# Setup, attention's first batch and the second feed-forward's beginning placed anew: a macaron block (feed-forward, attention, feed-forward) on one core

## The reference

```
x = x + 0.5 * ffn(layernorm(x))        # router, 8 experts of at most 320 tokens, overflow goes to a dense MLP
x = x + attn(layernorm(x))             # 16 heads of 16 channels, 1024 x 1024 scores per head and batch
x = x + 0.5 * ffn(layernorm(x))        # the same ffn weights again
```

```
ffn:  eid = argmax(softmax(xf @ router_w + router_b));  rank = place among the tokens of the same expert
      rank < 320: relu(xf @ w1[eid] + b1[eid]) @ w2[eid] + b2[eid]
      else:       relu(xf @ ow1 + ob1) @ ow2 + ob2
attn: xd = x @ W_down; keys, queries, values = per-head 16x16 maps of xd
      softmax(queries keys^T * scale) values, then @ W_unify + b_unify
```

## Time and profile before

| | us |
|---|---|
| median of three runs | 2703.88 (2700.58 to 2704.08) |
| the profiled execution | 2695.95 |
| its span | 2694.2 |
| PE, DVE, ACT, POOL busy | 2582.5, 2052.0, 1761.2, 915.1 |
| granted TensorE clock, mean | 0.983 of full |

### The profile page before, as it was taken

How to read it: one execution, slowest core, us unless ns; L and a number is a source line. 1 busy time by engine, 2 the same in 40 slices (tenths; PEclk the granted TensorE clock), 3 DMA queues, 4 the chain that set the end, 5 groups by cost and what they waited for, 6 DMA issues and landing times. The chain is left out here.

```text
span 2694.2 us, 46722 instructions
## 1 busy us (share of the span) xinstructions
PE 2582.5 (96%) x17379; PEld 1624.1 (60%) x17379; DVE 2052.0 (76%) x3471; ACT 1761.2 (65%) x3620; POOL 915.1 (34%) x975
## 2 busy tenths in 40 slices
PE   6999999977999999999999999999999699999998
PEld 6888899952344344443443443444444488888998
DVE  5656557847898998998998989979997266655586
ACT  4444446743787887887877878878878444444576
POOL 2333324632332342333323323422212143332364
PEclk9999999986999999999999999999999799999999
DMA  4421214515244143242351341432421332221353
GB/s 121 97 71 56 64 53 126 160 56 97 49 78 104 48 94 78 62 100 57 78 103 52 72 103 49 81 74 66 81 60 43 112 87 74 61 71 40 86 156 96
DMA packets 191811, 216.86 MB, mean 80 GB/s; under 512 B 56364, under 2 KB 152804, under 8 KB 191584
## 3 DMA queue, kind: packets, MB, share of 16 engines
q1 hardware_dynamic: 156176, 169.03, 26.9%
q0 software_dynamic: 35408, 44.84, 6.0%
HBM read 114.54 MB, written 48.57 MB: 61 GB/s over the span
## 5 line engine op out<-in xcount | busy, mean ns | idle before, releaser
L1397 DVE TENSOR_REDUCE at_mxc<-at_pb 128x2 f32<-128x1024 f32 x1024 | 1210.7, 1219 | 137.6 <-PE at_pb L1227 134.4
L1337 ACT ACTIVATE at_ex<-at_pd 128x512 f32<-128x512 f32 (+1 forms) x2418 | 1105.8, 539 | 303.9 <-PE at_pd L1237 293.1
L1237 PE MATMUL at_pd<-at_qa,at_ka 50*128 50x512 f32 (+1 forms) x2418 | 641.1, 406 | 4.3 <-ACT at_ex L1337 4.3
L1237 PEld LDWEIGHTS at_pd<-at_qa,at_ka 50*128 50x128 f32 x2418 | 317.9, 185 | 493.1 <-issue 404.5
L1227 PE MATMUL at_pb<-at_ka,at_qa 48*128 48x512 f32 x2048 | 551.5, 467 | 33.5 <-DVE at_mxc L1397 17.7
L699 ACT ACTIVATE f_ml_h<-f_ml_pL,b1T 128x512 f32<-128x512 f32 (+1 forms) x384 | 243.6, 634 | 493.5 <-PE f_ml_pL L763 493.4
L614 DVE TENSOR_TENSOR f_ml_hl<-f_ml_h,f_ml_hh 128x512 fp32r<-128x512 f32 (+1 forms) x384 | 279.4, 728 | 364.5 <-ACT f_ml_hh L702 363.5
L1246 PE MATMUL at_po<-at_ex,at_va 128*32 128x512 f32 x4096 | 546.3, 605 | 0.0
L776 PE MATMUL f_ml_pA<-f_wh,f_ml_hh 128*128 128x256 f32 (+1 forms) x1408 | 411.5, 292 | 0.0
L778 PE MATMUL f_ml_pA<-f_wl,f_ml_hh 128*128 128x256 f32 (+1 forms) x1408 | 396.8, 282 | 0.0
L779 PE MATMUL f_ml_pA<-f_wh,f_ml_hl 128*128 128x256 f32 (+1 forms) x1408 | 396.8, 282 | 0.0
(11 more groups left out here) (123 smaller groups left out, 2645.7 us busy)
## 6 DMA issues: line engine op xcount, KB each, us to landing
f_wraw<-in_L_ffn_w SPq DMA_DIRECT2D x128, 256.0 KB, 3.2
at_qa<-at_parts SPq DMA_DIRECT2D x384, 64.0 KB, 2.5
at_ka<-at_parts SPq DMA_DIRECT2D x384, 64.0 KB, 2.6
at_oscr<-at_os POOLq DMA_DIRECT2D x63, 256.0 KB, 2.4
f_ml_xr<-in_L_attn_x SPq DMA_DIRECT2D x16, 512.0 KB, 6.7
f_ml_xs<-in_L_attn_x SPq DMA_DIRECT2D x16, 512.0 KB, 4.4
x<-f_ml_yo SPq DMA_DIRECT2D x16, 512.0 KB, 5.3
at_xr<-x SPq DMA_DIRECT2D x16, 512.0 KB, 4.8
```

What stands on the lines that cost most here:

```text
L1237: eng.matmul(pd[n.bank][:, part.at], ka[g][rows, p, kt * P:(kt + 1) * P], qa[g][rows, qh, p, part.at], start=True, stop=True).then_inc(s_f ...
L1337: eng.activation(ex[t % 2][:, part.j, part.at], pd[n.bank][:, part.at], ACT.Exp).then_inc(s_free[n.bank].sem, 1)
L1397: eng.tensor_reduce(mxc[:, t // NT, kh, t % NT::NT], pb[kh][:, :].rearrange("p (e k) -> p e k", e=2), AX.X, ALU.max, negate=True).then_inc ...
```

## The change

**Setup goes into the first feed-forward's block.** `setup` only notes its inputs. In `mlps` with `setup` given, SP issues the first rows, one piece of the weights and only then the biases; the router's and attention's weights come behind. POOL makes the constants at the start of the same block, PE turns the biases into a half of a tile of pA, DVE copies them out between its first statistics and its first weights. `turned(u, f)` sends the second turn of the first block to pR, so that it doesn't wait for pT.

**The second feed-forward's start goes into attention's last batch.** A `Shared` set of tiles (rows, raw weights, high and low weights) serves both. Attention's xr and xT lie in the raw weights' tile, its xn and xd in the rows' tile, its parts in the high and low weights' tiles. In batch 7 SP loads the dense weights and the first 512 rows at unit 1, step 0 (`load_next`); POOL splits the eight pieces at steps 2, 3, 10, 11 of units 1 and 2 (`next_split`); DVE and POOL do statistics, power and normalising of the first rows at steps 7, 8, 9 and 11 of unit 3. The second `mlps` (`early = 1`) leaves all of that out.

**Attention's first batch.** The list becomes `XT + XD[:2] + QK[:2] + XD[2:] + V + QK[2:]`. Its qk is split straight out of PSUM: ACT writes the high part, DVE the low (`queries_low`); POOL splits only xd. Head 1 of unit 0 is loaded by ACT's queue, the others by SP's. `first` on PE does the maxima of steps 0 to 10, then the exponentials of step 0, then the maxima of steps 11 and 12.

```
-            stats(0)
-            weights(0, 0)
-            apply(0)
-            weights(0, 1)
+            if setup:
+                stats(0)
+                setup.copies(eng, pA[1][:, 1, :])
+                weights(0, 0)
+                apply(0)
+                weights(0, 1)
             for f in range(DT):
                 rows_low(0, f)
...
+        turned = lambda u, f: pR if (u, f) == (0, 1) else pT
...
-                sides = [self.place(task, 0, 0, 0, i % BANKS) for i, task in enumerate(XT + XD + QK[:2] + V + QK[2:])]
+                sides = [self.place(task, 0, 0, 0, i % BANKS) for i, task in enumerate(XT + XD[:2] + QK[:2] + XD[2:] + V + QK[2:])]
...
+        def load_head(eng, b, g, j, queries=()):
+            if b == 0:
+                eng.wait_ge(s_kp.sem, s_kp.at(len(XD) * (c + 1)))
+                for a in queries:
+                    if a.at[0] == c:
+                        eng.wait_ge(s_free[a.n.bank].sem, s_free[a.n.bank].at(a.n.freed))
...
+            def load_next():
+                eng.wait_ge(s_xn.sem, s_xn.at(2 * NBAT))
+                eng.wait_ge(s_kp.sem, s_kp.at(parts_ahead(NBAT)))
+                eng.wait_ge(s_pv.sem, s_pv.at(ST * unit(NBAT - 1, 1)))
+                for s in s_st:
+                    eng.wait_ge(s.sem, s.at(16 * 2))
+                for q in range(PIECES):
+                    load_weights(eng, shared.raw, q, *k.dense).then_inc(s_next.sem, 16)
+                eng.dma_start(shared.xr, o_t[:, 0:4, :]).then_inc(s_next.sem, 16)
...
         @block.scalar
...
                         side_out(a)
+                        if a.kind == "qk" and a.at == (0, 1):
+                            load_head(eng, 0, 0, 1, [a for a in sides if a.kind == "qk"])
...
+            def queries_low(a):
+                eng.wait_ge(s_qh.sem, s_qh.at(2 * c + f + 1))
+                eng.scalar_tensor_tensor(parts[0][:, 1, c, at], pd[a.n.bank][:, :], SCALE * SCALE, parts[0][:, 0, c, at].bitcast(F32),
+                                         ALU.mult, ALU.subtract).then_inc(s_free[a.n.bank].sem, 1)
...
         @block.vector
...
                         eng.memset(v[:, :, :, HS:VW], 1.0).then_inc(s_rc.sem, 1)
+                    for a in sides:
+                        if a.kind == "qk":
+                            queries_low(a)
                     stats(1, range(NT))
                     variance(1, range(NT))
...
+            def next_split(q):
+                if q == 0:
+                    eng.wait_ge(s_next.sem, s_next.at(16 * (PIECES + 1)))
...
+                eng.tensor_copy(shared.high[:, sl], shared.raw[:, sl]).then_inc(s_ws.sem, 1)
+                eng.wait_ge(s_ws.sem, s_ws.at(q + 1))
+                eng.tensor_tensor(shared.low[:, sl], shared.raw[:, sl], shared.high[:, sl].bitcast(F32), ALU.subtract)
```

More of the change, by code:

```diff
@@ L121, with setup @@
+def setup(nc, k, *inputs):
+    k.setup.of(*inputs)
 class Norm:
@@ L674, in _ @@
                 if g in EXPERTS:
+                    if setup and EXPERTS[g] == 0:
+                        setup.router_ready(eng)
                     route.experts_step(eng, EXPERTS[g])
@@ L805, in ffn @@
 def ffn(nc, k, name, x_in, x_out, w1, b2, w2, ow1, ow2, ob2):
+    begin, k.setup, k.dense = k.setup, None, (ow1, ow2)
     table = nc.dram_tensor(name + "table", (E * C, 1), I32).ap()
@@ L1192, in step @@
                         load_rows(2)
+                    if last and (g, t) == (1, 0):
+                        load_next()
                     if (g, t) == (3, 8) and b + 3 < NBAT:
@@ L1351, in side_out @@
                                              bank[:, i * D:(i + 1) * D].rearrange("p (h s) -> p h s", s=HS), ACT.Copy)
+                elif a.kind == "qk" and a.b == 0:
+                    c, f = a.at
+                    at = slice(f * 512, (f + 1) * 512)
+                    eng.activation(parts[0][:, 0, c, at], bank[:, :], ACT.Copy, scale=SCALE * SCALE).then_inc(s_qh.sem, 1)
+                    return
                 else:
```

337 lines of the change are left out of this document (210 added, 127 removed).

## The result

The changed kernel takes 2679.94 us (median of 4 runs, 2675.85 to 2684.21), the kernel before 2702.23 in the same session (4 runs, 2698.53 to 2704.08): a ratio of 0.9919, 95% interval 0.9899 to 0.9940. It is faster by 19 to 22 us. The forecast was 2680.2 with 23.7 us gained, and a range of 2674 to 2688.

A forecast was written before the change was run, and what follows sets the result against it. PE, busy 96% of the span, bounds the kernel; only three waits can shrink. 7.2 + 11.1 + 0.8 + 4.3 + 0.3 = 23.7 us, taken off the 2703.9 median, gives 2680.2, range 2674 to 2688.

The forecast's parts named there:

- 2% is far more than all three together could give: The three waits, at the program's start and attention's end and start, sum to some 50 us of 2694.
- Part 1: Program's start: setup inside the first feed-forward's block brings its first product forward, 7.2 us, bounds 6 to 7.5.
- The biases' copies: First feed-forward's start: DVE's two copies, 0.5 us together, hidden by POOL's power if the biases land by about 8.8.
- Part 2: Second feed-forward's start: loading, statistics and normalising go, so its first product comes 11.1 us sooner, with 0.8 behind it.
- The 0.8 behind it: Inside the second feed-forward: half of PE's 1.6 us wait for a late low part saved, 0 to 1.6.
- Part 3: Attention's first batch: first maximum 4.3 us sooner through earlier heads, plus 0.3 from a `first` two steps shorter.
- ACT's issue, the unknown: Attention's start: no row shows ACT's time per transfer; SP's 0.64 taken, so six transfers hold ACT 3.8 us.
- both rivals that priced it otherwise: Attention's start: ACT issues cheaply, 27.5 gained, 2676.4, chance 0.14; or issue costs double, 19.9 gained, 2684, chance 0.16.
- The text's own remark on slices 9 and 10: Profile page: PE's granted clock is full except in slices 9 and 10, where attention begins, and 32.
- So this costs nothing while POOL and SP have room: Attention's last batch: POOL's 15 us of splits, DVE's 3.4 us and SP's nine transfers add 0 us.
- steps longer than 2.56 us in the last batch: Attention's last batch: a sign that would show the forecast wrong.
- the one on POOL: Last batch: POOL's first split waits for nine transfers, over 60 us, delaying sums and PE; 2710, chance 0.02.

The follow-up runs named there:

- the second profile: The unedited changed kernel profiled again, in another session than its first: that run took 2680.19 us; the kernel's median there was 2676.65, ratio 0.9924.
- the first profile: The changed kernel's first profiled execution, with no further edit, the fastest of its four runs: 2675.85 us.
- the first session: The changed kernel, four runs beside the kernel before: 2679.94 us against 2702.23, ratio 0.9919.
- the other: Another session, the unedited changed kernel run again beside three edits: 2676.65 us (6 runs) against 2696.04 for the kernel before, ratio 0.9924.

## Why the prediction was right, and where it wasn't

The time, 2680.2, met 2679.94, and the mechanisms of the two feed-forwards' starts were right. That the time met to 0.3 us is luck: the gain was 22.3 us in place of 23.7, and the median of the kernel before, from which it was taken, came out 1.65 lower than the 2703.88 of the prediction. ("2% is far more than all three together could give" was also loosely read: its 50 of 2694 us are 1.9%.)

**Part 1, 7.2: 7.6.** SP's first transfer at 1.64 (1.40 forecast), the product at 13.67 (14.1). The biases' copies are hidden, as said. The tile's share was 1.74 us, not 1.4.

**Part 2, 11.1: 11.14**, of which the experiments without the early part and with the old setup give the shares: 8.74 the early part, 1.74 the second turn's tile, and 0.66 that neither accounts for. The 0.8 behind it was 0.95 in the second profile, but that stretch differs by 2.1 us among the eight profiles that have no odd waits, so it is neither shown nor refuted. PE's waits for turned rows' low parts went from 3.0 us to 2.6.

**Part 3, 4.3 + 0.3: 4.25 with the clock full, -0.34 with it low.** The chain was right link by link. ACT's issue, the unknown, took 0.68 each against the 0.64 taken from SP, so both rivals that priced it otherwise are out. DVE's statistics were what was late. What I left out is that ACT's hold leaves TensorE idle for 2.9 us in the middle of its side products, and that the granted clock may fall there. The text's own remark on slices 9 and 10 pointed at it. In four of seven profiles with this order it did fall, to between 0.50 and 0.66 in the five microseconds behind ACT's transfers, and the part was then worth 1.9 us to less than nothing, against 2.2 to 4.2 in the other three. Of two queues and one, one is at least as good: the second brings the first product of the heads 2.2 to 2.8 us forward with the clock full, and between 0.5 us forward and 1.0 back with it low, and for that holds for 4.1 us the engine that makes the rest of what the first maximum needs.

**The last batch, 0: -2.0 to -2.2, and -1.0 to -1.2 at its end.** This is the step that failed: "So this costs nothing while POOL and SP have room". Room was the wrong question. POOL had it, and what it ran there held DVE's three short operations for the length of its own; the normalising stood ahead of a reciprocal for which a chain of transfers waits, and TensorE behind it (0.97 and 1.20 us). In the table the second loss is hidden by the clock, which was full for both last products in the first profile and low for both in the second. The forecast asked for "steps longer than 2.56 us in the last batch" as a sign against it; there are two of them. Of its rivals only the one on POOL named this place, with another mechanism and some ten times the price.

So the forecast was 1.4 us too high in the first session and 4.3 in the other. The last batch's 3 us are in both. Where the clock fell, in the runs of either kernel, moves either figure by more than what is left; how much it moved each, only the profiled runs could say.

## What to carry to other kernels

Before calling work hidden because its engine is idle, look at which operations of the other engines run in the same microseconds: two engines that read the same memory can hold each other for whole operations, and a short one on the critical path then takes as long as the long one beside it. When a queue is given to a second engine, what that engine would have done in the issue time is the price. And an idle stretch of TensorE of three microseconds seems to cost twice: the second time through the clock, in some executions only (six of the nine profiles here). Take a second profile before a difference of 4 us is explained.

## What I had not expected of the hardware

One kernel's executions differed by 10 us in 2676 (2670.82 to 2681.10), and two profiles put 8.4 us of difference into two stretches with a granted clock of 0.50 or 1.00 for the same instructions. DVE's cast of 128x16 took 0.17 us alone and 0.54, 0.59 and 1.23 beside POOL; four `tensor_scalar` of 128x256 took 1.38 alone and 4.25 and 4.02 beside it. And more TensorE work in the lead gave the fastest attention start of all in one run, and runs of 14 to 21 us more in five.
